# Attention spread over 3.75 steps a pair, with its data kept in DRAM and its low parts on GpSimd

## The reference

```
x1 = x  + tanh(g_xattn) * xattn(layernorm(x), ctx, ctx)
x2 = x1 + tanh(g_ffn)   * ffn(layernorm(x1))

xattn: Q, K, V = per-head products with Wh (4 heads of 128)
       A = max(|sum over the batch of (Q K^T / sqrt(128)) * decay|, 1)   # one A per head for the whole batch
       O = A V;  Y = normalise(O) * gamma + beta;  result = (relu(x wg) * Y) wo
ffn:   g = (x gate^T) * gate_s;  u = (x up^T) * up_s;  out = ((silu(g) * u) down^T) * down_s     # inner size 1408
```

## Time and profile before

| | |
|---|---|
| runs of the kernel | 1558.38, 1556.02, 1556.26 us, median 1556.26 |
| the profiled execution | 1557.62 us |
| its span, first to last instruction | 1555.7 us |
| TensorE busy in the span | 1534.6 us (99%) |
| VectorE, ScalarE, GpSimd busy | 1101.5 us (71%), 477.7 us (31%), 273.0 us (18%) |
| granted TensorE clock | 0.999 |

### The profile page before, as it was taken

The page is one execution under the profiler, slowest core; times in us unless marked ns, Lnnn a source line. Parts: engine busy times, 40 slices in busy tenths (PEclk is TensorE's granted clock), DMA queues, the critical chain, the costliest instruction groups (busy, mean ns, idle before and its releaser), DMA issues.

```text
span 1555.7 us, 19826 instructions
## 1 busy us (share of the span) xinstructions
PE 1534.6 (99%) x7402; PEld 1286.7 (83%) x7402; DVE 1101.5 (71%) x1727; ACT 477.7 (31%) x723; POOL 273.0 (18%) x514
## 2 busy tenths in 40 slices
PE   6999999999999999999999999999999999999998
PEld 5888888887888888888888888888888888888887
DVE  6677777769777677777767676767676767777733
ACT  4444444443323222223222222223232222232221
POOL 3555545532000010100000101000000101010000
PEclk9999999999999999999999999999999999999999
DMA  7877777765644444443534443535344444444310
GB/s 242 275 256 275 270 237 246 248 203 164 177 115 114 104 123 115 108 125 106 141 89 142 100 133 88 135 82 136 94 123 115 115 107 120 115 105 124 81 40 28
DMA packets 339938, 222.40 MB, mean 143 GB/s; under 512 B 256960, under 2 KB 258112, under 8 KB 339648
## 3 DMA queue, kind: packets, MB, share of 16 engines
q1 hardware_dynamic: 339840, 221.11, 49.1%
HBM read 139.28 MB, written 90.44 MB: 148 GB/s over the span
## 4 chain that ended last, share of the span: by engine, by line
PE 94%; DVE 3%; DMA 1%; issue 1%; ACT 1%; SPq 0%; POOL 0%; DVEq 0%
PE ps L1179 60%; PE pyb L1079 16%; PE ps L1114 6%; PE po L1079 6%; PE ptb L1079 5%; PE ptb L1084 2%; DMA xr<-in_x 0%; DVE reg L653 0%; DMA raw<-v_scratch 0%; DMA wy_scratch<-misc 0%; DVE xn L612 0%; DVE tmp L753 0%; DVE st L665 0%; DVE misc L693 0%; DVE reg L617 0%
## 5 line engine op out<-in xcount | busy, mean ns | idle before, releaser
L1179 PE MATMUL ps<-reg,gate 128*128 128x512 f32 x1408 | 348.2, 389 | 0.0
L1179 PE MATMUL ps<-reg,up 128*128 128x512 f32 x1408 | 347.7, 389 | 0.0
L1179 PE MATMUL ps<-xreg,reg 128*128 128x512 f32 x1408 | 324.4, 389 | 0.0
L1179 PEld LDWEIGHTS ps<-reg,up 128*128 128x128 f32 x1408 | 264.3, 188 | 54.9
L1179 PEld LDWEIGHTS ps<-xreg,reg 128*128 128x128 f32 x1408 | 263.4, 188 | 54.1
L1179 PEld LDWEIGHTS ps<-reg,gate 128*128 128x128 f32 x1408 | 263.3, 188 | 53.9
L999 POOL TENSOR_SCALAR rs<-mv 128x1 f32<-128x1 f32 x192 | 45.4, 237 | 1171.0 <-DVE mv L667 592.9
L496 ACT ACTIVATE tmp<-ps,colsb 128x512 f32<-128x512 f32 x176 | 121.4, 690 | 392.1 <-PE ps L1179 392.1
L753 DVE SCALAR_TENSOR_TENSOR tmp<-ps,colsb,tmp 128x512 f32<-128x512 f32 x176 | 132.1, 750 | 148.3 <-PE ps L1179 145.4
L486 ACT CAST reg<-tmp 128x512 fp32r<-128x512 f32 x176 | 109.5, 622 | 330.2 <-DVE tmp L753 330.2
L1079 PE MATMUL pyb<-xreg,reg 128*128 128x512 f32 x720 | 178.4, 396 | 0.8 <-DVE xreg L629 0.8
(11 more groups left out here) (102 smaller groups left out, 1490.5 us busy)
## 6 DMA issues: line engine op xcount, KB each, us to landing
xr<-in_x SPq DMA_DIRECT2D x63, 512.0 KB, 5.1
raw<-in_ctx_t SPq DMA_DIRECT2D x32, 512.0 KB, 4.7
w_scratch<-tmp SPq DMA_DIRECT2D x64, 256.0 KB, 4.0
v_scratch<-tmp SPq DMA_DIRECT2D x64, 256.0 KB, 3.6
raw<-v_scratch SPq DMA_DIRECT2D x32, 512.0 KB, 4.6
raw<-w_scratch SPq DMA_DIRECT2D x64, 256.0 KB, 3.3
out<-xr SPq DMA_DIRECT2D x31, 512.0 KB, 3.0
wy_scratch<-misc SPq DMA_DIRECT2D x30, 512.0 KB, 3.0
```

What stands on the lines that cost most here:

```text
L1179: last = e.matmul(dst, l, r, start=(k == 0 and i == 0), stop=(k == n - 1 and i == 1))
```

## The change

1. The attention of pairs 2 to 31 is no longer tied to the group. Pair `q` begins at step `15 * (q - 2) // 4 - 1` of the whole FFN and has ten pieces, 0 to 9, one per step. Four pairs fall into each group and the last piece is at step 116 of 240, so no attention is left in the second half.
2. Since four pairs a group run ahead of the FFN, normalised `x1` (the FFN's input, "x2") stays in a DRAM scratch of 32 slots and is read back at steps 9 and 12 of the group before its own. `x1` is stored to DRAM as well (`x1_store`, piece 9) and read back into `xr` tiles 4 to 7 as the residual at step 4 (`residual`). `x2_blocks` writes a buffer of its own (`xbuf`). `turned[0]` serves only the first transpose, `turned[1]` only the second; there is one `wy_scratch`.
3. `hidden_lo`, `wy_pair_lo` and `v_lo` of pairs 3 and later (`v_pair_lo`) move from VectorE to GpSimd.

What each engine does in a step, in its order (`n` is the step, `pieces(n)` the pairs with a piece there, the older pair first):

```diff
+def first_step(q):
+    return 15 * (q - 2) // 4 - 1
+def pieces(n):
+    return [(q, n - first_step(q)) for q in range(2, B // 2) if 0 <= n - first_step(q) <= 9]
...
 # SyncE
+            def x1_store(q):
+                p.wait_ge("x1", 2 * q + 2)
+                e.dma_start(x1_s[:, 2 * q:2 * q + 2, :], xr[:, 2 * (q % 2):2 * (q % 2) + 2, :]).then_inc(s[f"x1s{q % 2}"], 16)
+            def wy_in(q):
+                p.wait_ge("wys", 16 * (q - 1))
+                if q > 2:
+                    p.wait_ge("wylo", q - 2)
+                blocks_in(wy_s, turned[0], "wyl")
...
+                    if step == 0 and g == 0:
+                        x1_store(0)
+                        x1_store(1)
+                    if step == 4:
+                        residual(2 * g)
+                        residual(2 * g + 1)
+                    for q, piece in pieces(15 * g + step):
+                        if piece == 3:
+                            wy_out(q)
+                            if q + 1 < B // 2:
+                                w_load(2 * q + 2)
+                                w_load(2 * q + 3)
+                            wy_in(q)
+                            if q + 2 < B // 2:
+                                v_load(q + 2)
+                        if piece == 4:
                             x_again(q)
+                        if piece == 9:
+                            x2_out(q)
+                            x1_store(q)
+                    if g + 1 < NG and step in (9, 12):
+                        x2_in(2 * g + (2 if step == 9 else 3))
...
 # ScalarE
                     if 1 <= step <= 11:
                         hidden_hi(11 * g + step - 1)
+                    for q, piece in pieces(15 * g + step):
+                        if piece == 1 and q + 1 < B // 2:
+                            v_hi(q + 1)
+                        if piece == 6:
                             wy_pair_hi(q)
+                    if g + 1 < NG and step in (11, 13):
+                        x2_pair_hi(2 * g + (2 if step == 11 else 3))
                     if step < 11:
                         silu(g, step)
...
 # VectorE
+                    if 1 <= step <= 11:
+                        hidden(g, step - 1)
+                    if step == 0 and g:
+                        finish(4 * g - 1)
+                    if step >= 12:
+                        finish(4 * g + step - 12)
+                    for q, piece in pieces(15 * g + step):
+                        t = 2 * q
+                        if piece == 8:
+                            norm2(t)
+                            norm2(t + 1)
+                            x2_blocks(t)
+                            x2_blocks(t + 1)
+                        if piece == 2:
+                            wy_blocks(t)
+                            y_second(t + 1)
+                            wy_blocks(t + 1)
+                        if piece == 1:
+                            y_stats(t + 1)
+                            y_scaled(t + 1)
+                            y_second(t)
+                    for q, piece in pieces(15 * g + step):
+                        t = 2 * q
+                        if piece == 0:
+                            y_stats(t)
+                            y_scaled(t)
+                        if piece == 7:
+                            x1(t)
+                            stats2(t)
+                            x1(t + 1)
+                            stats2(t + 1)
+                    if g + 1 < NG and step in (11, 14):
+                        x2_pair_lo(2 * g + (2 if step == 11 else 3))
...
 # GpSimd
+                    if 1 <= step <= 11:
+                        hidden_lo(11 * g + step - 1)
+                    for q, piece in pieces(15 * g + step):
+                        if piece in (0, 1):
+                            y_rstd(2 * q + piece)
+                        if piece == 2 and q + 1 < B // 2:
+                            v_pair_lo(q + 1)
+                        if piece == 6:
+                            wy_pair_lo(q)
+                        if piece == 7:
+                            rstd2(2 * q)
+                            rstd2(2 * q + 1)
...
 # TensorE
-                    p.wait_ge("tbwe", t + 1 if t < 4 else t // 2 + 3)
+                    p.wait_ge(*(("tbwe", t + 1) if t < 4 else ("wylo", t // 2 - 1)))
...
+                        for q, piece in pieces(15 * g + step):
+                            if piece == 0:
+                                o(q)
+                            if piece == 7:
+                                wo_mm(2 * q, range(4))
+                                wo_mm(2 * q + 1, range(4))
                         if step < 11:
                             up_mm(exact, g, step)
```

More of the change, by code:

```diff
@@ L12 @@
     ["xf", "eye", "whr", "whr2", "wgr", "cols", "rows", "dec", "wor", "wor3", "dld", "outb", "lowld", "vld"]
-    + [f"{name}{i}" for name in ("xl", "xa", "out") for i in range(4)]
-    + [f"{name}{i}" for name in ("ct", "vst", "wst", "wl", "wys", "wyl", "x2s", "x2l") for i in range(2)]
+    + [f"xl{i}" for i in range(4)]
+    + [f"{name}{i}" for name in ("ct", "vst", "wst", "wl", "xa", "x1s", "res", "out") for i in range(2)]
+    + ["wys", "wyl", "x2s", "x2l"]
     + [f"scr{c}" for c in range(12)] + [f"wld{c}" for c in range(8)]
@@ L249, in x_again @@
             def x_again(q):
-                if q >= 4:
-                    p.wait_ge(f"out{q % 4}", 16 * (q // 4))
-                elif q < 2:
+                if q >= 2:
+                    p.wait_ge(f"x1s{q % 2}", 16 * (q // 2))
+                else:
                     p.wait_ge("xn", 2 * q + 58)
@@ new lines, in wy_out, with x2_out, blocks_in @@
+            def wy_out(q):
+                p.wait_ge("wyb", 2 * q - 2)
+                if q > 2:
+                    p.wait_ge("wyl", 64 * (q - 2))
+                e.dma_start(wy_s.rearrange("t p n -> p t n"), tbuf).then_inc(s["wys"], 16)
+            def x2_out(q):
+                p.wait_ge("x2b", 2 * q - 2)
+                e.dma_start(x2_s[q].rearrange("t p n -> p t n"), xbuf[:, :, :]).then_inc(s["x2s"], 16)
+            def blocks_in(scratch, dst, name):
+                src = scratch.rearrange("t (u r) (c a j) -> a r c (t u) j", u=4, c=4, a=4)
+                for a in range(4):
+                    to = dst[32 * a:32 * a + 32, :, :].rearrange("r c (x j) -> r c x j", j=32)
+                    e.dma_start(to, src[a]).then_inc(s[name], 16)
@@ L402, in _ @@
             p.wait_ge("of", B - 1)
-            e.dma_start(out_v[:, B - 2, :], xr[:, (B - 2) % 8, :]).then_inc(s["outb"], 16)
+            e.dma_start(out_v[:, B - 2, :], xr[:, 6, :]).then_inc(s["outb"], 16)
             p.wait_ge("of", B)
-            e.dma_start(out_v[:, B - 1, :], xr[:, (B - 1) % 8, :]).then_inc(s["out3"], 16)
-            for i in range(4):
-                p.wait_ge(f"out{i}", 16 * (B // 8))
+            e.dma_start(out_v[:, B - 1, :], xr[:, 7, :]).then_inc(s["out1"], 16)
+            p.wait_ge("out0", 16 * (B // 4))
+            p.wait_ge("out1", 16 * (B // 4))
             p.wait_ge("outb", 16)
@@ L902, in _ @@
             e.tensor_scalar(ds, ds, tg[:, 1:2], None, ALU.mult).then_inc(s["ds"])
+            y_stats(4)
+            y_scaled(4)
             for g in range(NG):
[L906 to L915, removed]
@@ L976, in _ @@
-                finish(4 * g)
-                if more:
-                    v_lo(q + 2)
-                finish(4 * g + 1)
-                if more:
-                    y_stats(a + 4)
-                    y_scaled(a + 4)
-                if nxt:
-                    x2_pair_lo(q + 1)
-                finish(4 * g + 2)
-                if more:
-                    y_stats(a + 5)
-                    y_scaled(a + 5)
-                    v_lo(q + 3)
+                for step in range(15):
+                    if 1 <= step <= 11:
[31 more added lines that the diff above has]
+                        x2_pair_lo(2 * g + (2 if step == 11 else 3))
@@ L1023, in ct_split, with v_pair_lo, wy_pair_lo, hidden_lo @@
                 e.tensor_tensor(lo, raw[:, h, :], f(hi), ALU.subtract).then_inc(s["ctlo"])
+            def v_pair_lo(q):
+                p.wait_ge("vhi", q + 1)
+                e.tensor_tensor(vs_of(q)[1], raw[:, 0:2, :], f(vs_of(q)[0]), ALU.subtract).then_inc(s["vlop"])
+            def wy_pair_lo(q):
+                p.wait_ge("tbwh", q + 3)
+                e.tensor_tensor(wyt[1][:, :, :], turned[0][:, :, :], f(wyt[0][:, :, :]), ALU.subtract).then_inc(s["wylo"])
+            def hidden_lo(m):
+                p.wait_ge("hhi", m + 1)
+                e.tensor_tensor(hid[1][:, m % 11, :], tmp[:, m % 3, :], f(hid[0][:, m % 11, :]), ALU.subtract).then_inc(s["hlo"])
             e.memset(ones[:, :], 1.0).then_inc(s["ones"])
@@ L1059, in _ @@
             rstd2(3)
-            for g in range(1, NG):
-                a = 4 * g
-                y_rstd(a)
-                y_rstd(a + 1)
-                y_rstd(a + 2)
-                y_rstd(a + 3)
```

(18 more changed lines are left out.)

183 lines of the change are left out of this document (37 added, 146 removed).

## The result

The changed kernel takes 1687.92 us (median of 4 runs, 1685.91 to 1689.05) beside 1556.15 us for the kernel before: ratio 1.0842, 95% interval 1.0823 to 1.086. The forecast was 1683 us, in a range of 1610 to 1715. The profiled execution took 1685.91 us with a span of 1684.0, 128.3 us more than before.

What follows compares the result with a forecast made beforehand. TensorE's gapless matmul queue was taken as the bound, any wait lost in full. A 45.5, B 39.7, D 27.3, x2 1.4, clock 14, minus 1.2 make 126.7 us: 1683 us; range 1650 to 1715, with rivals 1610 to 1715.

Steps and rivals of the forecast that it cites:

- At most some 1.2 us can be won: In the second stage TensorE is a queue of matmuls without holes; the removed waits give 1.2 us.
- A: Pairs q = 2, 6, ... 30, begun at step 14 of the group before: wo_mm stalls 5.5 us, 45.5 with group 0.
- B: Pairs q = 3, ... 31, begun at step 2 of a group: wo_mm stalls 5.4 us each, 39.7 in sum.
- D: Pairs q = 5, 9, ... 29, begun at step 10 of a group: wo_mm stalls 3.9 us each, 27.3 in sum.
- C: Pairs q = 4, ... 28, begun at step 6 of a group: low part made at step 12, no stall.
- group 0: First group: late load of V of pair 4 holds v_hi and silu, 2.5 us, plus 4.5 at A.
- x2: Last subtraction waits on VectorE behind C's piece 8 and A's piece 0 at step 14: 0.2 us, seven times, 1.4.
- the one that comes second waits for the whole remainder: VectorE's two-SBUF-input y_second instructions and GpSimd's subtractions alternate; stall in step 8 grows from 4.0 to 5.4 us.
- rival 1: Two-input VectorE instructions do not collide with GpSimd's: +86.6, 1643 us; chance 0.25.
- the instruction of L730: Sign on VectorE: it would be stretched where GpSimd is busy, only in the first half.
- The clock: Granted clock falls in long stalls: 2 us on half of the 14 of A and B, 14 us; bounds 0 and 44.
- The extra 33.6 MB: More DMA, 64 tiles of 256 KB out and in, on engines busy 43%: costs nothing.

Runs made afterwards that it cites:

- experiment 6: Kernel before with only the third part of the change, hidden_lo, wy_pair_lo and v_lo from pair 4 on made by GpSimd: 1553.36 us, ratio 0.9976.
- experiment 1: Changed kernel with wy_pair_hi and wy_pair_lo ahead of hidden_hi and hidden_lo in the same step: 1605.79 us, ratio 1.0304.
- experiment 2: Changed kernel with wo_mm, x1, stats2 and rstd2 moved from piece 7 to 8, later pieces one step on: 1633.62 us, ratio 1.0488.
- experiment 5: Changed kernel with hidden_lo, wy_pair_lo and v_pair_lo back on VectorE: 1686.82 us, ratio 1.083.
- experiment 4: Changed kernel with VectorE's product W*Y replaced from tile 4 on by a 32 x 32 block transpose with one SBUF input: 1673.1 us.
- experiment 3: Changed kernel with extra matmuls, results thrown away, filling the waits ahead of wo_mm: 1658.35 us, ratio 1.0652.
- experiment 8: experiment 1 with v_pair_lo at piece 3 instead of 2 for pairs q = 3, 7, ..., and that of pair 3 at piece 1: 1581.72 us, ratio 1.0155.

## Why the prediction came out right

**The bound.** TensorE's queue sets the time; every wait was lost in full. Right, with one slip (in the section on what bounds the kernel): "At most some 1.2 us can be won" was wrong. About 4 us were to be had (experiment 6), in holes that the idle time of TensorE doesn't show and the row of weight loads does. The number was in the earlier trace rows too: 24 matmuls took 5.57 us there, where 24 x 0.227 are 5.45.

**The place.** `wo_mm` on GpSimd's `wyt` 23 times, at A, B and D and not at C, nothing in the second half: as forecast. Experiments 1 and 2 show that both of its causes count, the one step of distance and the order within the step; experiment 5 shows that the same waits come with VectorE in GpSimd's place.

**The size of the waits.** I had 113.9 us for A, B, D, group 0 and x2. Measured by the distances between starts: 4.7, 4.7 and 3.0 us at A, B and D (the named wait and 0.17 us that the modelled end hides) against 5.5, 5.4 and 3.9, none for x2, and 96 us in all. The term was too large by 18 us.

That the one that comes second waits for the whole remainder was right. In the timeline above L716 ends at 723.80 and L719 starts at 723.83; `hidden_lo` ends at 724.95, L719 at 725.50, `v_pair_lo` at 727.74. They alternate. Of the 15 L716 and 23 L719 that began under a long GpSimd instruction in this stage every one was stretched, L716 to between 1.05 and 2.26 us, L719 to between 1.64 and 1.67.

What was mis-sized is the time behind such a wait: I added an instruction's whole time, and it needs 0.1 to 0.2 us less (`hidden_lo` 1.15 for my 1.30, L719 0.55 for 0.69, `v_pair_lo` 2.24 for the 2.4 of its size). At B and D VectorE was also 0.2 to 0.5 us earlier than I had it. For B, counted from the start of step 8 at 747.22, `wy_pair_lo` ends at 8.28 and not 9.04. A's 5.5 us had no working behind them: 1.5 us added to 4.0, and 0.7 was measured.

That the collisions cost something is shown (experiment 4); rival 1, without them, gave 1643. One sign did not come: the instruction of L730 (now L749) was never stretched (0.55 us at most), as it never began under a long GpSimd instruction.

**The clock.** I charged 14 us, 2 us on half of 14 waits. It was about 30 (experiment 3). Of 24 waits 19 brought a stretch at half clock: all 16 of 3.4 us and more (A, B and `o`(3)), 3 of the 7 of 2.9 us (D), not the one of 1.6 (the last B). Each cost 1.6 to 1.7 us (4.44 us for twelve matmuls against 2.72, or 2.85 behind a wait at full clock; 29.6 us for the 18 that experiment 3 took away). The price was nearly right and the count, 7, was not. What I had taken from the end of the program, a fall 2.1 us after the last matmul, is near the shortest of what came here, 1.9 to 5.3 us. Even a fall that comes late costs in full, as it then lies on the work behind the wait.

**Group 0.** I had 7.0 us, from a late load of V of pair 4 and A. The sum was near (3.8 + 3.4 us) but the mechanism was `o`(3) on `v_pair_lo`, which I hadn't seen. The load is real: it was covered by that wait and came out in experiment 8.

The two large errors, 18 us too much for the waits and some 16 too little for the clock, cancel. The time was right to 0.3%, and that is luck; its terms were off by a fifth and by half. The upper end of the forecast's own range, 1715, does not follow from its terms: the clock's bound alone reaches 1713, and 1 us more on each of 22 stalls 1735.

**DMA.** The extra 33.6 MB were costed at nothing; experiment 8, with all of them, is 25 us above the kernel before. Some 9.5 of them are two waits in group 0 (1.4 and 5.3 us, by the starts 1.6 and 5.4) and 2.5 us of half clock. The six groups from `wo_mm` of A at 507.36 to that at 1048.03 take 90.1 us each, where their matmuls alone take 87.4 (59.9, 4 x 1.43, 4 x 5.45): 2.7 us a group, 19 over seven groups. The 4 us of holes that the kernel before has come off. The 2.7 us are short waits for `wyt`, 1.0 us at A and 0.3 to 1.1 at B or C, where VectorE and GpSimd are still behind, and a slower start of 0.1 to 0.2 us after each. The waits of that kernel hold no DMA but the load of V; no run takes the extra DMAs away alone, so it stays open whether they cost a part of the few microseconds left.

The best version is not the changed schedule at all but its third part alone in the old one: 0.24% faster than the kernel before (interval 0.15 to 0.34%).

## What to carry to other kernels

When one engine is busy 99% of the time, spreading or moving the others' work can win only its holes, and can lose any chain that no longer fits between two places of its queue: write down, for each producer, the queue in front of it and the time to its consumer's place, not the engine's share. When a wait goes, look at what stood behind it (`o` behind `wo_mm` in experiment 2, the load of V in experiment 8), and expect it to appear. Look for small holes of a matmul queue in the waits of the weight loads, and count the half clock with each wait of several microseconds.

## What the runs showed of the hardware

- In the kernel after, the granted clock fell 1.9 to 5.3 us after TensorE stopped, 9 times inside the wait and 10 times on the matmuls behind it. Example: TensorE stood from 726.8 to 731.3 at 1.00, then the clock was 0.50 from 731.9 to 735.3. Waits of 4.5 us always brought it, of 2.9 us in three of seven, one of 1.6 us did not. In experiment 5 waits of 2.1 us brought it in five of seven, in experiment 1 waits of 3.3 us in four of six.
- 393 extra matmuls in waits made a kernel 29.6 us faster.
- VectorE's product of two SBUF operands took up to 1.67 us beside a GpSimd subtraction, alone 0.69; a 32 x 32 block transpose in its place 0.71. In the kernel after all 38 of VectorE's two-operand instructions of `y_second` that began under a long GpSimd instruction were stretched, and none of 75 block transposes (0.72 us at most). GpSimd's subtraction of 1024 elements took 2.34 us alone and 2.8 beside it; of 512, 1.26 and 1.67.
